# Projection stage: the queries' normalization steps of three batches, on GpSimd instead of VectorE

## What is computed

```python
def _ln(t, w, b):
    m = jnp.mean(t, axis=-1, keepdims=True)
    v = jnp.var(t, axis=-1, keepdims=True)
    return (t - m) * jax.lax.rsqrt(v + EPS) * w + b
...
q = _ln((x @ Wq + bq).reshape(b, s1, H, HD), qn_w, qn_b)
kv = jnp.concatenate([y_main @ Wk + bk, y_main @ Wv + bv], axis=-1)
kv = kv.reshape(b, s2, H, 2 * HD)
k = _ln(kv[..., :HD], kn_w, kn_b)
v = kv[..., HD:]
```

## Time and profile before

| | before |
|---|---|
| time, median of 3 runs | 2177.82 us (2176.29 to 2178.30) |
| time of the profiled execution | 2179.09 us |
| its span | 2177.3 us |
| projection stage in it | about 505 to 692 us |
| busy over the span | PE 1900.2, DVE 1248.4, POOL 1018.6, ACT 576.1 us |

### The profile page before, as it was taken

The page is one execution under the profiler, slowest core; times in us unless marked ns, Lnnn a source line. Parts: engine busy times, 40 slices in busy tenths (PEclk is TensorE's granted clock), DMA queues, the critical chain, the costliest instruction groups (busy, mean ns, idle before and its releaser), DMA issues. The chain is left out here.

```text
span 2177.3 us, 33697 instructions
## 1 busy us (share of the span) xinstructions
PE 1900.2 (87%) x10056; PEld 1386.7 (64%) x10057; DVE 1248.4 (57%) x2365; ACT 576.1 (26%) x1291; POOL 1018.6 (47%) x560
## 2 busy tenths in 40 slices
PE   5965788796888668999879999999999999999995
PEld 3433444563333223333359989999999999999995
DVE  1556354447676766777476445555555555555542
ACT  2330122420112335444322312222222222222221
POOL 0000000000654646565405776555555677689886
PEclk9987898798998779999989999999999999999998
DMA  3024210412124355760114675666556666778999
GB/s 122 1 74 121 78 33 20 153 40 92 61 94 149 115 186 188 240 218 24 45 42 151 221 239 172 167 186 179 164 162 168 200 176 191 201 195 198 222 185 192
DMA packets 274088, 308.30 MB, mean 142 GB/s; under 512 B 40920, under 2 KB 185304, under 8 KB 274008
## 3 DMA queue, kind: packets, MB, share of 16 engines
q1 hardware_dynamic: 147096, 190.48, 27.7%
q10 hardware_dynamic: 105408, 65.80, 11.4%
q0 software_dynamic: 21504, 50.93, 10.1%
HBM read 188.58 MB, written 118.55 MB: 141 GB/s over the span
## 5 line engine op out<-in xcount | busy, mean ns | idle before, releaser
L2561 PE MATMUL psum<-e_gu_high,e_rowT_high 128*128 (+1 forms) x1272 | 425.4, 336 | 7.6 <-ACT e_rowT_high L2240 2.8
L2561 PE MATMUL psum<-e_gu_low,e_rowT_high 128*128 (+1 forms) x1272 | 409.9, 325 | 0.0
L2566 PE MATMUL psum<-e_gu_high,e_rowT_low 128*128 (+1 forms) x1272 | 256.2, 323 | 0.0
L2561 PEld LDWEIGHTS psum<-e_gu_high,e_rowT_high 128*128 128x128 f32 x1272 | 241.2, 190 | 20.6 <-issue 14.7
L2561 PEld LDWEIGHTS psum<-e_gu_low,e_rowT_high 128*128 128x128 f32 x1272 | 241.7, 190 | 6.3
L2240 ACT CAST e_rowT_high<-psum 128x512 fp32r<-128x512 f32 x127 | 74.5, 586 | 615.9 <-DVE psum L2324 615.9
L2566 PEld LDWEIGHTS psum<-e_gu_high,e_rowT_low 128*128 128x128 f32 x1272 | 213.6, 189 | 0.0
L2363 DVE COPY f_arena<-psum 128x512 f32<-128x512 f32 x127 | 87.8, 692 | 189.8 <-PE psum L2586 189.8
L2581 PE MATMUL psum<-e_d_high,e_midT_high 128*128 (+3 forms) x477 | 188.5, 395 | 0.6 <-ACT e_midT_high L2246 0.6
L2581 PE MATMUL psum<-e_d_low,e_midT_high 128*128 (+3 forms) x477 | 187.8, 394 | 0.0
L2194 POOL DMA_INDIRECT X<-d_y,f_slots x96 | 150.4, 1566 | 37.3 <-issue 26.2
(11 more groups left out here) (384 smaller groups left out, 3799.8 us busy)
## 6 DMA issues: line engine op xcount, KB each, us to landing
d_sorted<-f_hs SPq DMA_DIRECT2D x32, 1048.0 KB, 9.8
d_y<-f_arena ACTq DMA_DIRECT2D x127, 256.0 KB
f_arena<-d_sorted ACTq DMA_DIRECT2D x484, 64.0 KB, 2.5
f_gu_in<-in_L_ffn_w_gate SPq DMA_DIRECT2D x32, 704.0 KB, 5.4
f_gu_in<-in_L_ffn_w_up SPq DMA_DIRECT2D x32, 704.0 KB
f_d_in<-in_L_ffn_w_down SPq DMA_DIRECT2D x32, 512.0 KB, 4.1
d_y<-f_hs SPq DMA_DIRECT2D x8, 1024.0 KB, 5.8
f_d_in<-in_L_ffn_w_down SPq DMA_DIRECT2D x32, 192.0 KB, 4.6
```

The costliest lines, as they stand in the source:

```text
L2561: nc.tensor.matmul(bank[:, 0:M].unsqueeze(1), rowT_high[par][:, k, :], w[:, bass.ds(buffer, 1), k, at:at + M], start=(k == 0 and n == 0), ...
L2566: last = nc.tensor.matmul(bank[:, 0:M].unsqueeze(1), rowT_low[par][:, k, :], gu_high[:, bass.ds(buffer, 1), k, at:at + M], start=False, st ...
```

## The change

For batches 0 to 2 the three steps that finish the queries go from DVE to POOL, behind the keys' power of the same batch. POOL's steps are 128 x 2048 each, with the same operands. DVE's `sum_squares` of the next queries, which overwrites the queries' half of `x_hrstd`, now waits for `q_scaled`; the scaled weights and offsets have a semaphore of their own, since POOL reads them.

```diff
+        affine_ready, q_normed, q_weighed = sems(nc, c, "x_", "affine_ready q_normed q_weighed")
...
+            def finish_q(b):
+
+                tile = by_head(q[b % 2][:].rearrange("p j n -> p (j n)"))
+                pool.wait_ge(affine_ready, 1)
+                pool.wait_ge(hrstd_ready, b * 2 + 1)
+                wide = (P, JT * H, HD)
+                nc.gpsimd.tensor_tensor(tile, tile, hrstd[:, 0, :].unsqueeze(2).broadcast_to(wide), ALU.mult).then_inc(q_normed, 1)
+                pool.wait_ge(q_normed, b + 1)
+                nc.gpsimd.tensor_tensor(tile, tile, affine[:, 0, 0, :].unsqueeze(1).broadcast_to(wide), ALU.mult).then_inc(q_weighed, 1)
+                pool.wait_ge(q_weighed, b + 1)
+                nc.gpsimd.tensor_tensor(tile, tile, affine[:, 0, 1, :].unsqueeze(1).broadcast_to(wide), ALU.add).then_inc(q_scaled, 1)
+
             for b in range(B - 1):
                 power(b, 0)
                 power(b, 1)
+                finish_q(b)
             power(B - 1, 0)
...
-            chain.link(nc.vector.tensor_scalar(affine[:, 0], affine[:, 0], SCALE, None, ALU.mult))
+            nc.vector.tensor_scalar(affine[:, 0], affine[:, 0], SCALE, None, ALU.mult).then_inc(affine_ready, 1)
+            dve.wait_ge(affine_ready, 1)
...
                     if j == JT // 2:
+                        if b >= 1:
+
+                            dve.wait_ge(q_scaled, b)
                         sum_squares(b, 0)
...
                 if b < B - 1:
                     sum_squares(b, 1)
-                    finish(b, 0, q[par][:], q_scaled)
                     add_bias(b)
                     finish(b, 1, k[par][:], k_scaled)
```

## The result

The changed kernel takes 2213.07 us (median of 4 runs, 2211.2 to 2215.15), the kernel before beside it 2178.06 (4 runs, 2176.29 to 2180.52): ratio 1.0154, 95% interval 1.014 to 1.0167. (The ratios given here are those on record, which differ a little from the quotient of the two medians.) By the medians the change is 35.0 us slower; 38.9 had been forecast.

What follows compares the result with a forecast made beforehand. Bound: the projection stage's chain of keys' power on POOL, keys' steps and copies on DVE, then PE. 11.4 us per batch, 34.2 for three, plus 4.7 for the clock gave 38.9: 2216.7 us, range 2203 to 2230.

Steps and rivals of the forecast that it cites:

- What bounds the stage: Projection stage, between batches: keys' power on POOL, keys' steps and copies on DVE, then PE; queries' steps off this chain.
- the handover's 0.14: DVE and POOL instructions holding each other: each handover saves about 0.14 us of the follower's own length.
- Who is first: At the keys' power's end POOL's step starts before DVE's, then they alternate; chance 0.60.
- The rival with DVE first: DVE gets in first at the power's end, only two POOL steps hold the keys: 2209.2 us; chance 0.28.
- The keys' steps: On DVE beside POOL's three steps: 19.9 us from power to `k_scaled` instead of 7.00, cost 12.9 per batch.
- POOL's price: Length of each of the three wide steps moved to POOL: 4.54 us, 13.6 for three; bounds 4.51 and 5.1.
- The clock: TensorE's eight matmuls before the third key tile slow after longer idling: 2.35 us each in batches 1 and 3, 4.7 together.
- The new waits: Waits of `sum_squares` for `q_scaled` and on the scaled weights, and the queries' store by SP: all cost nothing.
- The rival "no holding": Keys' steps take their 7.00 us beside POOL, only the power's gain remains: 2171.9 us, faster; chance 0.08.
- the first rival: The rival with DVE first; it had the next rows held by POOL's third step at 0.46 us per 512 columns.
- The rule named in the prediction: DVE and GpSimd share a lock on a port pair: the second to issue waits until the first is done.

Runs made afterwards that it cites:

- e5_swap: Kernel before the change, with the residual's bias moved ahead of the queries' steps on DVE: 2171.91 us, ratio 0.9973; timed again 2172.36 and 2168.94.
- e2_late: Changed kernel, POOL's three steps waiting for the keys' steps, sum of squares only for the first of the three: 2202.19 us, ratio 1.0115 to the kernel before.

## Why the prediction was right

- *What bounds the stage* held: the queries' three steps lay beside the power on DVE, and taking them away won nothing but the power's 1.6 us (10.93 instead of 12.52; forecast 1.5); DVE waits 8.51 us for the power instead of 3.38. The power went in behind the first of the four bias instructions, as taken: it is 0.38 longer than the 10.55 of the queries' power, and the first instruction ends about 0.5 after the power's start, which less the handover's 0.14 is the same. e5_swap shows that this gain needed no work on POOL.
- *Who is first* held: POOL's step starts 0.02 to 0.04 us before the power ends, DVE 0.03 to 0.04 after it, in all three batches. The Trainium skill's rule in "GPSIMD Engine Reference", section "Instruction dispatch", gives the same order. The rival with DVE first appears in none of the three batches. (It was also priced with held rows in all three; behind the third there are no rows, only the memset and the selector's copy, so its 2209.2 was up to 1.9 too high.)
- *The keys' steps*: forecast 19.9 us, measured 18.96. The term that was mis-sized is POOL's price. I took 4.54 three times and bounded the step with one number per head from 4.51 to 5.1; it takes 3.64, below the lower bound, and 0.9 of the 0.94 lies there. With the prices of e2_late, 7.00 + 3.64 + 4.56 + 4.55 - 5 x 0.14 = 19.05.
- *The clock*: forecast 2.35 each in batches 1 and 3. Batch 1 gave 2.62 and batch 2 another 0.3, both inside the bounds; in batch 3 the eight matmuls took 1.5 more, but only 0.5 reached the end of the stage. There the term was mis-sized: 2.35 was taken, and it wasn't asked what waits behind. In the kernel before, DVE still idled 0.86 us for PE ahead of 687.65; in the change it doesn't idle there, which takes up most of the other 1.0.
- *The new waits* cost nothing, as said: POOL's third step ends at 588.89, and DVE comes to the sum of squares that waits for it only at 598.36, without having been idle.
- *The rival "no holding"* falls with the L982 rows: 5.72 against 2.29 with the repeated operand. That the rows are held as the first rival had it, too, e2_late shows.

The stage grew by 34.46 us where 38.9 had been forecast, 4.4 less. Three times 1.07 of it lie in the batches (11.4 forecast, 10.33 measured), mostly in POOL's cheaper first step; 1.25 lies in the clock (4.7 forecast; 2.62, 0.30 and 0.53 measured). Taken as a whole both terms were too high, so neither hid the other's error.

## What to carry to other kernels

Moving elementwise work from a half-idle VectorE to a half-idle GpSimd is priced in two ways: by its length there, and by every VectorE instruction on SBUF that runs beside it, each of which can wait out a whole GpSimd instruction. Look in the trace for the same pair side by side before moving anything, and at what the critical engine does during that time: instructions with an input in PSUM (2.48 us for four, beside GpSimd or not) and reductions (2.27) can stand beside GpSimd, the long elementwise steps on SBUF can't. And where a GpSimd instruction like the power here, long but on few numbers, is on the path, see that no long VectorE instruction starts just ahead of it: one line moved gained 6 to 9 us here, in three timings.

## What was not expected

- A GpSimd step whose second operand is one number repeated 32 times is cheaper than one that reads a row of 32 numbers again and again: 3.64 against 4.56 us for 128 x 2048.
- Of two DVE instructions with no wait between them, the second can lose its place to a waiting POOL instruction: L991 took 4.98 us behind L990, for 0.68.
- One-input row instructions with per-row operands were held too: four of them, 1.91 us together, took 11.51 beside POOL's three steps.
- The power, 10.55 us long, leaves DVE alone in its middle: L982 and L988 took 2.28 and 4.62 there. Only what runs at its start (by up to 1.97 us) or at its end (by 0.3) lengthened it. The rule named in the prediction, that the second to issue waits until the first is done, fits the elementwise steps but not the power.
